# Batch attention in a fused kernel: four late output buffers instead of two, and the next stage's first rows normalised earlier at both joints

## The chip, the cores and the metric

The kernel runs on one NeuronCore of a Trainium2 chip. The metric is the device time of one launch in microseconds (us); the lower the better. The core has five engines that run their own instruction streams and meet only at semaphores: TensorE (PE, matmuls and transposes), VectorE (DVE), ScalarE (ACT), GpSimd (POOL) and SyncE (SP, which here issues every DMA).

## The reference, cut to what matters

Six layers run one after the other on x of 16 sequences by 512 rows by 256 columns. The first three (expert feed-forward, dilated attention, expert feed-forward) are not touched. The last three are a channel mix, an attention across the batch, and the channel mix again:

```python
x = x + 0.5 * channel_mix(layernorm(x))
x = x + batch_attention(layernorm(x))
x = x + 0.5 * channel_mix(layernorm(x))

def channel_mix(x):                      # 16 sequences, 512 x 256
    x_prev = shift_down_one_row(x)
    xr = mu_r * x + (1 - mu_r) * x_prev
    xk = mu_k * x + (1 - mu_k) * x_prev
    return sigmoid(xr @ W_r.T) * (square(relu(xk @ W_k.T)) @ W_v.T)

def batch_attention(x):
    q, k, v = x @ Wq.T, x @ Wk.T, x @ Wv.T
    scores = q @ k.reshape(b, d, s) / sqrt(d)
    attn = softmax(scores, axis=0)       # over the 16 sequences
    return where(tril, attn, 1e-9) @ v
```

## The kernel before, in words

The three last layers are one block of code, `mix_and_attend`: channel mix c1, batch attention b1, channel mix c2. Each engine gets one long instruction stream with all three, written out by hand, and nothing but semaphores orders the engines. So at a joint between two stages the order of the lines in each engine's stream decides what waits for what.

A "row" n of a channel mix is one sequence, 512 x 256 floats or 512 KB, held as 4 tiles of 128 rows; there are 16. c1 keeps five buffers of input (`RING`), two of output. For each row DVE takes mean and variance (`statistics`, or `front` in c2), POOL makes the reciprocal root (`root`), the row is scaled (in c1 and c2 by ACT, in b1 by DVE's `scale`), and PE transposes it (`turn_h`). In c1 DVE then runs `mixed`, `square` and `output` and PE runs `keys`, `receptance`, `values`. `output` writes first "rk" and then "y"; PE's `values(n)` waits for "rk" of row n-1, since both use one bank of PSUM.

The joint c1 to b1. Near the end of c1's loop on SP, at turn n == B - 2 = 14 and so behind the store of row 13, `open_sync` of b1 issues the load of b1's row 0, the weights, rows 1 and 2 and three constants. On DVE the loop of c1 ends with `square(15)`, `output(14)`. Then come b1's `open_vector` (two memsets, `statistics(0)`, `scale(0)`, `weight(0)`, `turned(0)`, `statistics(1)`) and c1's `output(15)`. PE, after `receptance(15)`, runs b1's `turn_h(0)`, then c1's `values(15)`, then b1's `query(0)`, `key(0)`, `turn_h(1)`. ACT turns the transposed row into its upper half (`turned`, L1984), DVE subtracts to get the lower (L2055).

b1 has a first part (16 rows: queries, keys, values), ten score blocks (`weigh` on DVE and POOL), and 32 output groups (`outputs` on PE, `output` on DVE, L2140). A group is 128 query rows of two sequences, 128 x 512 floats, 256 KB. The list `groups` has query block 3 (groups 0 to 7), block 2 (8 to 15), the first five of block 1 (16 to 20), and then blocks 0 and 1 mixed: group 21 is block 0, sequences 0 and 1; 22 is block 0, sequences 2 and 3; 23, 26 and 29 are block 1; the rest block 0. For each group DVE waits for the matmuls (a ring of four PSUM slots), for the residual `xo` read back from x_c, and for the store that last used its `yt` buffer. It adds and writes `yt`. SP's `put` then stores `yt` and at once loads the residual of group n + 2 into the `xo` buffer just freed. There are two buffers of each kind, so the residual of group n is asked for only when group n - 2 is done. PE's `outputs(n)` waits for DVE's output n - 4. Groups of block 0 also wait for POOL's `gather(1, g)` of the same sequences (L2038), which waits for PE's group of block 1 of these.

The joint b1 to c2. Behind store 17, SP issues c2's identity, mu and three weights (`load_weights`). Behind store 23 come c2's rows 0 and 1 (row 0 needs the landed store of group 21), behind 24 rows 2 and 3, behind 26 row 4. DVE runs outputs up to 25, `rests`, `front(0)`, outputs 26 and 27, `weight(0)`, `front(1)`, outputs 28 and 29, `mixed(0)`, outputs 30 and 31, `weight(1)`, and then c2's `front(2)`, `mixed(1)`. PE runs `outputs` to 28, c2's `turn_h(0)`, outputs 29 to 31, `turn_h(1)`, `keys(0)`. POOL runs gathers 0 to 5 of block 1, `root(0)`, gather 6, `root(1)`, gather 7.

`at` is a list of six blocks of 16 x 128 floats a partition (the attention weights). Score block n uses `at[n % 6]`, so `at[4]` and `at[5]` hold blocks 4 and 5, both of query block 2. They are read for the last time in the outputs of groups 8 to 15.

Of the kernel before, what the change touches and what calls it, by code (L numbers as in the profile page):

```python
# [14 lines left out]
B, S, D = 16, 512, 256  # L15
# [764 lines left out]
def channel_mix(nc, sems, name, src, dst, w, prior=None):  # L780

    stage = Stage()
    with ExitStack() as ctx:
        m = Memory(nc, ctx, name, sems)
# [59 lines left out]
        def sync(sp, after=None):  # L844
            for n in range(B):
                if after and n == B - 2:
                    after.open_sync(sp)
                d_out.wait(sp, at_(n), "y")
                sp.dma_start(row_tiles(dst, at_(n)), yt[n % 2][:]).then_inc(s_st[n % 2].sem, 16)
                if n + RING < B:  # L850
                    load(sp, n + RING)
            for k in range(2):
                sp.wait_ge(s_st[k].sem, 16 * (B // 2))
# [185 lines left out]
        def front(dve, n):  # L1039
            slot_wait(dve, s_ld, at_(n))  # L1040
            if n >= 2:
                a_h.wait(dve, at_(n - 2))
            norm.statistics(dve, at_(n))
# [48 lines left out]
        def vector(dve, after=None):  # L1092
            front(dve, 2)
            for n in range(B):
                if n + 1 < B:
                    mixed(dve, n + 1)
                square(dve, n)
                if n + 3 < B:
                    front(dve, n + 3)
                if n:  # L1100
                    output(dve, n - 1)
            if after:
                after.open_vector(dve)
            output(dve, B - 1)
# [589 lines left out]
def batch_attention(nc, sems, name, src, dst, w, prior):  # L1694

    stage = Stage()
    with ExitStack() as ctx:
# [18 lines left out]
        at = [m.sbuf(f"at{j}", B, P) for j in range(AT)]  # L1716
        yt = [m.sbuf(f"yt{k}", GB, D) for k in range(2)]
        q_blk = m.sbuf("q_blk", B, DC, P)
        mx, rc, rt = (m.sbuf(k, P) for k in ("mx", "rc", "rt"))
# [3 lines left out]
        tri, fill, unseen = (m.sbuf(k, P) for k in ("tri", "fill", "unseen"))  # L1723
        xo = [m.sbuf(f"xo{k}", GB, D) for k in range(2)]
        norm = Norm(m, NB, lambda t: xt[t.step % 3], half)
        p_s = m.psum("p_s", B, P)
# [12 lines left out]
        s_q = [m.track(f"s_q{k}", inc=16) for k in range(4)]  # L1739
        s_x, s_y = ([m.sem(f"s_{n}{k}") for k in range(2)] for n in "xy")  # L1740
        t_hT, a_hT, d_hT = m.track("t_hT"), m.track("a_hT"), m.track("d_hT")
# [17 lines left out]
        group_of = {group: n for n, group in enumerate(groups)}  # L1759
        HB = B // 2  # L1760

        def rows_of(a, n):
            qb, g = groups[n]
            return a.rearrange("(b s) d -> s b d", b=B)[qb * P:(qb + 1) * P, g * GB:(g + 1) * GB, :]
# [5 lines left out]
        def load_x(sp, n):  # L1770
            sp.dma_start(xo[n % 2][:], rows_of(src, n)).then_inc(s_x[n % 2], 16)

        def stored(sp, row):
            n = group_of[0, row // GB]
            sp.wait_ge(s_y[n % 2], 16 * (n // 2 + 1))

# [10 lines left out]
        def sync(sp, after):  # L1787
# [20 lines left out]
            def put(some):  # L1808
                for n in some:
                    d_y.wait(sp, at_(n))  # L1810
                    sp.dma_start(rows_of(dst, n), yt[n % 2][:]).then_inc(s_y[n % 2], 16)
                    if n + 2 < NB * G:
                        load_x(sp, n + 2)

            queries_for(2)
# [6 lines left out]
            after.load_weights(sp)  # L1822
            put(range(18, 24))
            after.load(sp, 0)
            after.load(sp, 1)
            put(range(24, 25))
            after.load(sp, 2)
# [3 lines left out]
            put(range(27, NB * G))  # L1831
            for k in range(2):
                sp.wait_ge(s_y[k], 16 * (NB * G // 2))

# [234 lines left out]

        def open_vector(dve):  # L2070
            dve.memset(unseen[:], UNSEEN).then_inc(s_z, 1)
            dve.memset(half[:], -0.5).then_inc(s_z, 1)
            statistics(dve, 0)
            scale(dve, 0)
            weight(dve, 0, wq)
            turned(dve, 0)
            statistics(dve, 1)

        def vector(dve, after):
# [54 lines left out]
            def output(some):  # L2134
                for n in some:
                    t_o.wait(dve, at_(n))
                    dve.wait_ge(s_x[n % 2], 16 * (n // 2 + 1))
                    if n >= 2:
                        dve.wait_ge(s_y[n % 2], 16 * (n // 2))
                    d_y.mark(dve.tensor_tensor(yt[n % 2][:], p_o[:, n % RING], xo[n % 2][:], ALU.add))  # L2140

# [12 lines left out]
            after.clear(dve)  # L2154
            output(range(18, 26))
            after.rests(dve)
            after.front(dve, 0)
            output(range(26, 28))
            after.weight(dve, 0)
            after.front(dve, 1)  # L2160
            output(range(28, 30))
            after.mixed(dve, 0)
            output(range(30, NB * G))
            after.weight(dve, 1)

    stage.stored, stage.scores_read, stage.outputs_read = stored, scores_read, outputs_read
    stage.open_sync, stage.open_tensor, stage.open_vector = open_sync, open_tensor, open_vector
# [110 lines left out]
```

## Time and profile before

| what | us |
|---|---|
| median of 3 runs (4042.88 to 4046.23) | 4043.06 |
| the profiled execution's own time | 4039.7 |
| its span, first to last instruction | 4037.8 |
| PE busy in it | 3821.2 (95%) |
| DVE / ACT / POOL busy in it | 3203.9 / 3070.6 / 2280.1 |
| mean granted TensorE clock (1 is full) | 0.984 |

The times at the start of rows below are us from the span's start. A row of a timeline gives start, length, engine, line, operation, what it writes and reads, how many instructions were merged, and in brackets how long the engine stood idle before it and what ended that. c1 ends and b1 begins near 3510; b1 ends and c2 begins near 3870.

### The profile page before, as it was taken

Reading aid. Unit: us, or ns where it says so; the run is one execution under the profiler, and the core shown is the slowest. Engines: PE = TensorE matmul, PEld = TensorE weight load, DVE = VectorE, ACT = ScalarE, POOL = GpSimd, SP = SyncE. Lnnn points to the kernel's source line nnn. Section 1 sums busy time; section 2 is a strip of 40 time slices with the busy share of each in tenths; the row PEclk is TensorE's granted clock in tenths of the full one; section 3 lists DMA queues with packets and bytes.
Section 4 is the critical chain, followed back from the end, with each engine's and each line's share of the span. In section 5 each row is a group of like instructions: output and inputs, shape, how many; then the busy total and the mean of one; then the engine's idle time right before and its main releaser. Section 6 shows DMA issues by size and latency. Waiting matters only on the chain. (4 is left out here: it accounts for less than half of the span.)

```text
span 4037.8 us, 82429 instructions
## 1 busy us (share of the span) xinstructions
PE 3821.2 (95%) x29464; PEld 3342.0 (83%) x29464; DVE 3203.9 (79%) x7740; ACT 3070.6 (76%) x7818; POOL 2280.1 (56%) x1818
## 2 busy tenths in 40 slices
PE   7999999999889999999998799999999988999989
PEld 6888888888768888888887688888888877898878
DVE  7888888888668787878876788888888867756567
ACT  6888888888678888888886688888888867632166
POOL 7888888888611111111100788888888866512356
PEclk8999999999989999999999899999999998999999
DMA  2000000000010000000000200000000002331342
GB/s 65 16 17 17 17 17 17 17 17 17 21 37 12 23 13 23 12 23 12 23 7 12 70 17 17 17 17 17 17 17 17 17 16 93 124 101 58 123 147 89
DMA packets 135064, 141.99 MB, mean 35 GB/s; under 512 B 8672, under 2 KB 131968, under 8 KB 134656
## 3 DMA queue, kind: packets, MB, share of 16 engines
q1 hardware_dynamic: 134656, 136.71, 10.6%
q8 instruction: 236, 3.87, 0.4%
q14 instruction: 172, 1.41, 0.1%
HBM read 80.06 MB, written 56.62 MB: 34 GB/s over the span
## 5 line engine op out<-in xcount | busy, mean ns | idle before, releaser
L300 POOL TENSOR_TENSOR f_grid<-f_sim 128x1024 f32<-128x1024 f32 x512 | 968.5, 1908 | 0.0
L1483 ACT ACTIVATE a_ex<-a_p_s,a_mneg 128x128 f32<-128x128 f32 x2048 | 726.4, 408 | 149.9 <-DVE a_mneg L1537 149.9
L686 DVE SCALAR_TENSOR_TENSOR f_p_u<-f_grid,f_te,f_p_dot 128x1024 f32<-128x1024 f32 x512 | 652.9, 1275 | 112.6 <-PE f_p_dot L106 66.1
L308 POOL TENSOR_TENSOR f_q<-f_q 128x1024 f32<-128x1024 f32 x256 | 607.2, 2383 | 123.1 <-ACT f_q L558 120.6
L695 DVE SCALAR_TENSOR_TENSOR f_q<-f_p_u,f_rz,f_grid 128x1024 f32<-128x1024 f32 x512 | 650.5, 1270 | 0.4
L539 ACT ACTIVATE f_grid<-f_grid,f_negm 128x1024 f32<-128x1024 f32 x512 | 559.5, 1143 | 0.0
L1483 ACT ACTIVATION_READ_ACCUMULATOR a_ex<-a_p_s,a_mneg 128x1 f32 x2048 | 507.2, 248 | 0.0
L443 PE MATMUL f_p_y<-f_eup,f_wT 128*128 128x256 f32 x2048 | 472.9, 379 | 0.0
L438 PE MATMUL f_p_y<-f_wdn,f_hs 128*128 128x256 f32 x2048 | 468.3, 382 | 0.0
L443 PEld LDWEIGHTS f_p_y<-f_eup,f_wT 128*128 128x128 f32 x2048 | 388.6, 190 | 57.6
L438 PEld LDWEIGHTS f_p_y<-f_wdn,f_hs 128*128 128x128 f32 x2048 | 378.9, 190 | 49.5
L1263 POOL TENSOR_TENSOR a_xb<-a_xt,a_bos 128x256 f32<-128x256 f32 x64 | 45.1, 736 | 577.3 <-DVE a_yt L1575 567.6
L1537 DVE TENSOR_REDUCE a_mneg<-a_p_s 128x4 f32<-128x512 f32 x512 | 330.3, 663 | 4.8 <-PE a_p_s L1337 4.8
L1543 DVE COPY a_exT<-a_p_s 128x512 f32<-128x512 f32 x384 | 261.0, 683 | 80.6 <-PE a_p_s L1348 79.1
L425 PE MATMUL f_p_wT<-f_ident,f_q 128*128 128x128 f32 x2048 | 269.2, 274 | 21.8 <-POOL f_q L308 20.4
L425 PEld LDWEIGHTS f_p_wT<-f_ident,f_q 128*128 128x128 f32 x2048 | 229.2, 141 | 44.3 <-POOL f_q L308 34.6
L552 ACT ACTIVATE f_hs<-f_p_hid 128x512 f32<-128x512 f32 x256 | 151.7, 593 | 141.6 <-PE f_p_hid L106 140.8
L1348 PE MATMUL a_p_s<-a_ident,a_ex 128*128 128x128 f32 x1536 | 244.5, 283 | 10.2 <-ACT a_ex L1483 4.8
L558 ACT ACTIVATE f_q<-f_q 128x2048 f32<-128x2048 f32 x128 | 244.3, 1908 | 0.0
L287 POOL TENSOR_TENSOR f_cand<-f_tx,f_ty 128x512 f32<-128x512 f32 x128 | 136.8, 1069 | 148.8 <-DVE f_ty L650 148.6
L1348 PEld LDWEIGHTS a_p_s<-a_ident,a_ex 128*128 128x128 f32 x1536 | 167.7, 141 | 56.5 <-ACT a_ex L1483 40.1
L546 ACT COPY f_wT<-f_p_wT 128x512 f32<-128x512 f32 x256 | 148.3, 579 | 76.5 <-PE f_p_wT L425 76.5
(622 smaller groups left out, 10448.3 us busy)
## 6 DMA issues: line engine op xcount, KB each, us to landing
x_f<-f_yt SPq DMA_DIRECT2D x64, 256.0 KB, 2.2
f_xt<-x SPq DMA_DIRECT2D x32, 256.0 KB, 2.9
a_xt<-x_f SPq DMA_DIRECT2D x16, 512.0 KB, 3.9
x_a<-a_yt SPq DMA_DIRECT2D x16, 512.0 KB, 2.9
f_xt<-x_a SPq DMA_DIRECT2D x32, 256.0 KB, 2.9
c_xt<-x_f SPq DMA_DIRECT2D x16, 512.0 KB, 4.9
x_c<-c_yt SPq DMA_DIRECT2D x16, 512.0 KB, 3.2
b1p_xt<-x_c SPq DMA_DIRECT2D x16, 512.0 KB, 3.9
```

What stands on the lines that cost most here:

```text
L300: g_grid.mark(pool.tensor_tensor(grid[v][:, hd, :].rearrange("p (i j) -> p i j", i=XROWS), sx[:, hd, :].unsqueeze(2).to_broadcast([P, XROW ...
L308: g_pair.mark(pool.tensor_tensor(q[v][:, 2 * k, :], q[v][:, 2 * k, :], q[v][:, 2 * k + 1, :], ALU.add), f"{v}{k}")
L425: last = pe.matmul(p_wT[:, e, :], q[v][:, hd, (k * HALF + e) * P:(k * HALF + e + 1) * P], ident[:], is_transpose=True, start=hd == 0, stop ...
L438: pe.matmul(p_y[:, v, :], hs[t.step % 2][:, e, v * P:(v + 1) * P], wdn[:, e, :], start=e == 0, stop=False)
L443: last = pe.matmul(p_y[:, v, :], wT[v][:, e, :], eup[:, e, :], start=False, stop=e == EC - 1)
L539: a_exp.mark(act.activation(grid[v][:, hd, :], grid[v][:, hd, :], ACT.Exp, bias=negm[:, v, hd:hd + 1]), f"{v}{hd}")
L686: d_mask.mark(dve.scalar_tensor_tensor(out=p_u[:], in0=grid[v][:, hd, :], scalar=te[:, v, hd, TOP - 1:TOP], in1=p_dot[:], op0=ALU.is_ge, o ...
L695: d_mul.mark(dve.scalar_tensor_tensor(out=q[v][:, hd, :], in0=p_u[:], scalar=rz[:, v, hd:hd + 1], in1=grid[v][:, hd, :], op0=ALU.mult, op1 ...
L1348: last = pe.transpose(p_e[i][:, n, :], ex[t.step % 2][:, i, n, :], ident[:])
L1483: last = act.activation(ex[t.step % 2][:, i, n, :], p_s[i][:, n, :], ACT.Exp, bias=mneg[:, i, n:n + 1], accum_out=z[t.step % 2][:, i, n:n ...
L1537: d_max.mark(dve.tensor_reduce(mneg[:, i, :], p_s[i][:], AX.X, ALU.max, negate=True), str(i))
L1543: d_ex.mark(dve.tensor_copy(exT[t.step % 2][:, i, :, :], p_e[i][:]), str(i))
```

## The change: what it does

It has three parts. First, two more buffers for outputs (`yt`) and two more for residuals (`xo`) are laid in the halves of `at[4]` and `at[5]`. Groups 0 to 15 use two buffers as before; from group 16 (`WIDE`) on, group n uses buffer n % 4. Behind the store of group 15 SP loads the residuals of 17, 18 and 19, and from 16 on the residual of n + 4. Second, at the joint of c1 and b1 `open_sync` runs one turn of SP earlier (behind the store of row 12), and the memsets, `statistics(0)` and `scale(0)` move on DVE ahead of c1's `output(14)`, as `first_row`. Third, at the joint of b1 and c2 SP asks for c2's rows 0 and 1 behind store 22 instead of 23, and for rows 2 and 3 behind store 24 as before. DVE runs `rests` behind output 23, `front(0)` behind 24, `weight(0)` and `front(1)` behind 26, `mixed(0)` behind 29 as before.

```diff
@@ channel_mix, sync
-                if after and n == B - 2:
+                if after and n == B - 3:
                     after.open_sync(sp)
@@ channel_mix, vector
                 if n + 3 < B:
                     front(dve, n + 3)
+                if after and n == B - 1:
+                    after.first_row(dve)
                 if n:
                     output(dve, n - 1)
@@ batch_attention
+        yt += [at[4][:, 4 * k:4 * k + 4].rearrange("p (g x) s -> p g (x s)", g=GB) for k in range(2)]
+        xo += [at[5][:, 4 * k:4 * k + 4].rearrange("p (g x) s -> p g (x s)", g=GB) for k in range(2)]
-        s_x, s_y = ([m.sem(f"s_{n}{k}") for k in range(2)] for n in "xy")
+        s_x, s_y = ([m.sem(f"s_{n}{k}") for k in range(4)] for n in "xy")
+        WIDE = 2 * G
+        buffer = [n % 2 if n < WIDE else n % 4 for n in range(NB * G)]
+        uses = [buffer[:n].count(buffer[n]) for n in range(NB * G)]
         def stored(sp, row):
             n = group_of[0, row // GB]
-            sp.wait_ge(s_y[n % 2], 16 * (n // 2 + 1))
+            sp.wait_ge(s_y[buffer[n]], 16 * (uses[n] + 1))
             def put(some):
                 for n in some:
                     d_y.wait(sp, at_(n))
-                    sp.dma_start(rows_of(dst, n), yt[n % 2][:]).then_inc(s_y[n % 2], 16)
-                    if n + 2 < NB * G:
+                    sp.dma_start(rows_of(dst, n), yt[buffer[n]][:]).then_inc(s_y[buffer[n]], 16)
+                    if n < WIDE:
                         load_x(sp, n + 2)
+                    if n == WIDE - 1:
+                        load_x(sp, n + 3)
+                        load_x(sp, n + 4)
+                    if WIDE <= n < NB * G - 4:
+                        load_x(sp, n + 4)
-            put(range(18, 24))
+            put(range(18, 23))
             after.load(sp, 0)
             after.load(sp, 1)
-            put(range(24, 25))
+            put(range(23, 25))
             after.load(sp, 2)
             after.load(sp, 3)
-        def open_vector(dve):
+        def first_row(dve):
             dve.memset(unseen[:], UNSEEN).then_inc(s_z, 1)
             dve.memset(half[:], -0.5).then_inc(s_z, 1)
             statistics(dve, 0)
             scale(dve, 0)
+
+        def open_vector(dve):
             weight(dve, 0, wq)
             turned(dve, 0)
             statistics(dve, 1)
@@ batch_attention, vector, end
             after.clear(dve)
-            output(range(18, 26))
+            output(range(18, 24))
             after.rests(dve)
+            output(range(24, 25))
             after.front(dve, 0)
-            output(range(26, 28))
+            output(range(25, 27))
             after.weight(dve, 0)
             after.front(dve, 1)
-            output(range(28, 30))
+            output(range(27, 30))
             after.mixed(dve, 0)
             output(range(30, NB * G))
             after.weight(dve, 1)
```

The waits in `load_x`, `output` and at the end of `sync` are changed in the same way to `buffer` and `uses`.

## Rows read from the trace of the kernel before

**Rows 1.** Timeline of VectorE at the joint of c1 and b1.
```profile
3504.06 1.22 DVE L1069 TENSOR_TENSOR c_ks<-c_relu,c_p_k 128x1024 f32<-128x1024 f32 x1 [4.17 <-ACT c_relu L1001]
3506.46 1.23 DVE L1076 SCALAR_TENSOR_TENSOR c_rk<-c_p_v,c_rs 128x1024 f32<-128x1024 f32 x1 [1.18 <-PE c_p_v L936]
...
3508.92 0.17 DVE L2071 MEMSET b_unseen<- 128x128 f32 x1
...
3510.51 0.38 DVE L128 BATCH_NORM_AGGREGATE b_mv<-b_bs 128x2 f32<-128x6 f32 x4
3512.43 1.38 DVE L145 TENSOR_SCALAR b1p_h<-b1p_xt,b_mv,b_rstd 128x256 f32<-128x256 f32 x4 [1.53 <-POOL b_rstd L137]
3513.73 0.68 DVE L2068 TENSOR_TENSOR b1p_wql<-b_q_blk,b1p_wqh 128x512 fp32r<-128x512 f32 x1
3516.98 1.22 DVE L2055 TENSOR_TENSOR b1p_hT0l<-b_p_s,b1p_hT0h 128x1024 fp32r<-128x1024 f32 x1 [2.57 <-ACT b1p_hT0h L1984]
```
**Rows 2.** Timeline of TensorE at the same joint.
```profile
3513.95 1.94 PE L1841 MATMUL b_p_s<-b_ident,b1p_h 128*128 128x128 f32 x8 [4.73 <-DVE b1p_h L145]
3515.69 4.14 PE L936 MATMUL c_p_v<-c_wv,c_ks 128*128 128x256 f32 x16
...
3523.02 0.39 PE L104 MATMUL b_p_o<-b1p_wkl,b1p_hT0h 128*128 128x256 f32 x1 [0.45 <-DVE b1p_wkl L2068]
```
**Rows 3.** SyncE's DMA issues: when b1's first row was asked for.
```profile
3500.33 0.51 SPq L1768 DMA_DIRECT2D b1p_xt<-x_c  x1
```
**Rows 4.** Waits from 3820 to 3890: us in total, times, longest us.
```profile
DVE b_yt L2140 <- DMA b_xo<-x_c: 23.6, 12, 5.1
```
**Rows 5.** Windows: PE, PEld, DVE, ACT, POOL busy (count); PE clock, DMA share, GB/s.
```profile
3834.00:3839.00 5.00, 2.95 (x14) 2.27 (x12) 0.00 (x0) 0.62 (x1) 2.69 (x3) 1.00 0.96 307
3851.00:3859.00 8.00, 1.98 (x10) 1.81 (x10) 2.43 (x9) 2.07 (x4) 2.93 (x5) 0.73 1.06 363
```
**Rows 6.** SyncE's DMA issues near the joint of b1 and c2.
```profile
3833.33 0.47 SPq L1771 DMA_DIRECT2D b_xo<-x_c  x1
...
3834.45 0.92 SPq L1771 DMA_DIRECT2D b_xo<-x_c  x1
...
3846.65 1.07 SPq L825 DMA_DIRECT2D c_xt<-x_b  x2
```
**Rows 7.** Timeline of VectorE at that joint.
```profile
3839.00 0.69 DVE L2140 TENSOR_TENSOR b_yt<-b_p_o,b_xo 128x512 f32<-128x512 f32 x1 [5.07 <-DMA b_xo<-x_c]
3840.32 0.69 DVE L2140 TENSOR_TENSOR b_yt<-b_p_o,b_xo 128x512 f32<-128x512 f32 x1 [0.62 <-DMA b_xo<-x_c]
...
3850.95 1.41 DVE L124 BATCH_NORM_STATS2 c_bs<-c_xt 128x6 f32<-128x256 f32 x4 [0.72 <-DMA c_xt<-x_b]
...
3864.07 0.74 DVE L1060 SCALAR_TENSOR_TENSOR c_xk<-c_p_tr,c_mu,c_oldk 128x512 f32<-128x512 f32 x1
...
3868.41 0.69 DVE L2140 TENSOR_TENSOR b_yt<-b_p_o,b_xo 128x512 f32<-128x512 f32 x1 [1.02 <-DMA b_xo<-x_c]
3869.02 1.65 DVE L1052 TENSOR_TENSOR c_wrl<-c_raw,c_wrh 128x512 fp32r<-128x512 f32 x1
```
**Rows 8.** Timelines of TensorE, GpSimd and ScalarE at that joint.
```profile
3857.22 1.94 PE L899 MATMUL c_p_tr<-c_ident,c_h 128*128 128x128 f32 x8 [6.02 <-issue]
...
3862.81 0.59 PE L1943 MATMUL b_p_o<-b_v_all,b_at 128*128 128x256 f32 x2
...
3866.02 0.67 PE L1943 MATMUL b_p_o<-b_v_all,b_at 128*128 128x256 f32 x2 [1.32 <-POOL b_v_all L2038]
...
3864.60 1.27 POOL L2038 TENSOR_TENSOR b_v_all<-b_v_all 128x512 f32<-128x512 f32 x1
...
3866.66 1.03 ACT L995 CAST c_xk0h<-c_xk 128x1024 fp32r<-128x1024 f32 x1
```
**Rows 9.** DMA issues: KB each, us to landing; c2's first load alone.
```profile
c_xt<-x_b SPq DMA_DIRECT2D x1, 512.0 KB, 4.3
```
**Rows 10.** The chain that ended last: PE's transposes of c2's third row.
```profile
3878.48 1.93 PE c_p_tr L899 x8
```

More of the change, by code:

```diff
@@ L1770, in load_x @@
         def load_x(sp, n):
-            sp.dma_start(xo[n % 2][:], rows_of(src, n)).then_inc(s_x[n % 2], 16)
+            sp.dma_start(xo[buffer[n]][:], rows_of(src, n)).then_inc(s_x[buffer[n]], 16)
         def stored(sp, row):
             n = group_of[0, row // GB]
-            sp.wait_ge(s_y[n % 2], 16 * (n // 2 + 1))
+            sp.wait_ge(s_y[buffer[n]], 16 * (uses[n] + 1))
         def open_sync(sp):
@@ L1831, in sync @@
             put(range(27, NB * G))
-            for k in range(2):
-                sp.wait_ge(s_y[k], 16 * (NB * G // 2))
+            for k in range(4):
+                sp.wait_ge(s_y[k], 16 * buffer.count(k))
         def turn_h(pe, n):
@@ L2136, in output @@
                     t_o.wait(dve, at_(n))
[L2137 to L2140, printed above, removed]
+                    dve.wait_ge(s_x[buffer[n]], 16 * (uses[n] + 1))
+                    if uses[n]:
+                        dve.wait_ge(s_y[buffer[n]], 16 * uses[n])
+                    d_y.mark(dve.tensor_tensor(yt[buffer[n]][:], p_o[:, n % RING], xo[buffer[n]][:], ALU.add))
             for n in range(5):
@@ L2164, in vector @@
             after.weight(dve, 1)
-    stage.stored, stage.scores_read, stage.outputs_read = stored, scores_read, outputs_read
+    stage.stored, stage.scores_read, stage.outputs_read, stage.first_row = stored, scores_read, outputs_read, first_row
     stage.open_sync, stage.open_tensor, stage.open_vector = open_sync, open_tensor, open_vector
```

## The prediction

> **What bounds the kernel now.** I read the page first: PE is busy 95% of the span, so only moments when PE waits can be won. The chain that ended last runs through PE almost everywhere in the last three stages, and leaves it at two places, the two joints that the change touches. I then read each joint on the timelines of DVE, PE, SP, POOL and ACT, and the windows for the DMA share.
>
> At the first joint PE stands 4.73 us until DVE has scaled b1's first row [rows 2]. On DVE the reader is to see an idle 1.18 us behind `square(15)`, then `output(14)`, and only then the memset that opens b1 at 3508.92 [rows 1]. Row 0 had been asked for at 3500.33 [rows 3] and was there: the memset and the statistics stand back to back behind `output(14)`.
>
> At the second joint DVE waited 12 times and 23.6 us in all for residuals [rows 4]. These waits look like the price of two buffers: a residual is asked for only when the output two groups before is done. But the windows say something else as well. From 3834 to 3839 the 16 DMA engines are at a share of 0.96, from 3851 to 3859 at 1.06 [rows 5]. For much of the joint the transfers wait for each other, not for a buffer. So the 23.6 us are no measure of the gain; what ends last is c2's row 0, which lands just before 3850.95 [rows 7].
>
> **First joint, step by step.** Asking for row 0 one turn earlier (one row of c1, about 10 us) costs SP ten issues in a stretch where it waits for DVE anyway; it stands ahead of store 13, which is not due for another 10 us. Cost nothing; without that cover, some 0.5 us an issue [rows 3], so 5 us, and onto a store nobody waits for.
>
> `first_row` can start when `square(15)` ends, at 3504.06 + 1.22 = 3505.28, so 3.65 us before 3508.92 [rows 1]. Statistics, POOL's root and the scale follow as before, with POOL idle at that time: the scaled row is ready at 3510.15 and not 3513.81. PE's transposes start then (its `receptance(15)` ends at 3509.2: 3513.95 less the idle 4.73 [rows 2]), ACT's upper half and DVE's `turned(0)` follow. Now what it is moved past: `output(14)` takes DVE 2.46 us (3506.46 to 3508.92) and starts at 3510.15. With `weight(0)` (0.6 to 0.7) it fills DVE until 3513.3. `turned(0)` stood at 3516.98 and can come at 3516.98 - 3.65 = 3513.33 [rows 1]. So `output(14)` lies just inside the hole in which DVE waited for ACT (2.57) and in the old 1.53 wait for POOL, less the 1.18 it had in front. Behind it waits PE's `values(15)`, for "rk" of row 14, written at about 3511.4. The transposes end between 3511.2 (at their usual 0.9 to 1.0) and 3512.1 (at the 1.94 of the row), so 0.2 us or nothing is lost there, and PE has slack, because `key(0)` waits for DVE (0.45) [rows 2]. Gain: 3.65 us. Bounds: 3.0 if "rk" and the queue on DVE cost more than the hole, 4.5 if PE, which now idles one us and not 4.73, doesn't run its transposes and `values(15)` slowly (4.14 for the latter [rows 2], 3.45 as usual) and that reaches the path.
>
> **Second joint.** Residuals 18 and 19 are now asked for behind store 15, before 3815, when nothing else is moving. Groups 16 to 19 therefore pass at once, and 20 and 21 take over the places of 18 and 19 in SP's order. The weights come behind store 17 in both kernels. So the residual loads issued at 3833.33 and 3834.45 [rows 6] are those of 22 and 23 and no longer of 20 and 21, and they land when they did, near 3838.95 and 3840.3, when DVE could take its two outputs [rows 7]. This is the backlog that four buffers don't shorten. The gain in groups is two.
>
> After that the backlog goes on where before it ran dry. A 256 KB transfer costs 0.65 us in it (one store and one load between the two outputs, 1.32 us [rows 7]); at the 363 GB/s of [rows 5] 262 KB take 0.72. I take 0.7. SP issues store 20, load 24, store 21, load 25 in one go behind load 23, as their outputs were done by 3834. In order they land at 3841.0, 3841.7, 3842.4 and 3843.1. Output 22 is at 3838.95, so store 22 and load 26 are issued by 3840.6. Then SP stands in `load(0)` until store 21 has landed: 3842.4, and issues c2's row 0 at 3842.45, before it was 3846.65 [rows 6]. Ahead of it are load 25, store 22, load 26 (2.1 us), so it is there at 3844.5 + 1.4 = 3845.9 at the earliest; with the 4.3 us it took before [rows 9], at 3846.75. I take the later: `front(0)` starts 4.2 us earlier than 3850.95. DVE is free by then (output 24 is done near 3842.5). What is queued behind `front(0)` on DVE are outputs 25 and 26 with residuals that landed long before. They wait some 4 us for nothing; their stores and loads 29 and 30 come later by that, and land by 3857, before PE has group 29.
>
> From `front(0)` the chain to PE's `turn_h(0)` is POOL's root, ACT's scale, 6.27 us [rows 7, 8]: 3853.0 in place of 3857.22. PE stands as before, some 6 us. Group 29 then is ready at 3858.6 (3862.81 less 4.2 [rows 8]). Here a second wait goes. POOL's last gather started at 3864.60, behind `root(1)`, though group 29 was ready at 3862.81; and PE's group 31 waited 1.32 for it [rows 8]. Now `front(1)` stands ahead of outputs 27 to 29, so `root(1)` is over by 3855, the gather starts at 3858.65, ends at 3859.9, and PE goes straight on. Group 31 starts at 3866.02 - 4.2 - 1.32 = 3860.5, so it is 5.5 us earlier. On DVE `mixed(0)` comes behind output 29, at 3859.3 (before 3864.07), output 31 at 3862.6 (before 3868.41), `weight(1)` at 3863.3 (before 3869.02): 5.7. ACT's cast of xk0 depends on `mixed(0)` and no longer on the scale of row 1: 3861.3, before 3866.66, so 5.35 [rows 7, 8]. The join of both, PE's `turn_h(2)` at 3878.48 [rows 10], moves by the smaller. From there PE runs row on row, and the gain reaches the end. I take 5.4 us. Bounds: row 0 landing at 3845.9 gives 6.2; landing as late as before leaves only the 1.3 of the gather.
>
> **Rule and row.** The Trainium skill ("DMA: Bandwidth & Descriptors", section Specifications) puts HBM at about 358 GB/s for one core, and the trace at 363 GB/s agrees, hardly above it. By that rule 256 KB take 0.73 us and the sum hardly moves. The same page (Queues, rings and completion order) says descriptors are consumed in ring order, but that completion isn't strictly in order between issues. If the transfers were shared and not served in order, load 22 would be held up by the four transfers now issued behind it; what this gives is the first rival.
>
> **The sum.** 3.65 + 5.4 = 9.05 us. The profiled execution took 4039.7, so it would take 4030.7, span 4028.8. It was 3.4 under the median of the runs, so I set the difference against the median: 4043.06 - 9.05 = 4034.0. The parts between the joints issue the same instructions; two loads move into an empty time of the DMA engines.
>
> **The rivals.** *The DMA engines eat the second gain.* At shares of 0.96 to 1.06 a deeper queue only makes each transfer wait longer. If row 0 lands at 3851 in spite of the earlier issue, the second joint gives 1.3 and the sum is 4.95: 4038.1. For it: those shares. Against: the share is low between 3839 and 3841, when SP had only just been given new work, and row 0 lies behind a fixed number of bytes. Chance 0.22. *The first joint gives nothing:* `output(14)` behind `scale(0)` holds PE's `values(15)` and `turned(0)` as long as the earlier start saves. It would need 3.65 us where I count 0.2. The sum is 5.4: 4037.7. Chance 0.10. *The change does nothing,* since waits elsewhere take it back: 4043. Chance 0.07. *Slower:* `front(0)` at the head of DVE's queue waits for a row that itself waits for store 21 in a full queue; outputs 25 on, and PE's group 29, stand behind it. Each us of row 0's landing costs one. The other gains (3.65 and 1.3) are gone when it lands at 3855.9, and over 0.2% are lost at 3864. That needs 13 to 21 us from issue to landing, where the row shows 4.3. 4052. Chance 0.03.
>
> **How the numbers follow.** A measurement of this kernel can tell about 0.2%, 8.1 us, from no change. My forecast, 4034.0, is just past it; its own range is 4030.5 to 4037 (joint sums 12.5 to 6: the bounds of both joints, and 1 us of scatter), with a chance of 0.58, and about a tenth of the whole lies in that range but under 8.1 us. Faster by over 0.2%: 0.52, within: 0.44, slower: 0.04. The range, to hold 8 in 10, takes in the first two rivals: 4030 to 4039.5.
>
> **What would show it.** In the trace of the changed kernel: PE's idle before L1841 at the first joint at one us, the memset right behind `square(15)`, `output(14)` behind the scale, and `key(0)` 3.65 us earlier. At the second joint: no wait before outputs 18 and 19, a wait of over 4 us before output 22, no row under a share of 0.8 from 3829 to 3850, L825's first issue near 3842.5 - 3.65 and `front(0)` 4.2 us + 3.65 earlier than 3850.95, PE's group 31 with no wait for POOL. I am wrong if row 0 takes over 6 us to land, or if `turn_h(1)` and `keys(0)` wait for something that I didn't list.

## The result, and the profile after

| | kernel before | changed kernel |
|---|---|---|
| median of 8 runs, us | 4043.62 (4037.59 to 4047.96) | 4032.12 (4027.77 to 4038.89) |
| span of the profiled execution, us | 4037.8 | 4027.7 |
| ratio of the runs | | 0.9972, 95% interval 0.9962 to 0.9983 |

The changed kernel is 0.28% faster: 4043.62 x 0.0028 = 11.3 us, 6.9 to 15.4 by the interval. The two profiled executions differ by 10.1 us. Forecast were 9.05 us and 4034.0.

The first joint on VectorE after the change, beside [rows 1]:

```profile
3504.14 1.22 DVE L1069 TENSOR_TENSOR c_ks<-c_relu,c_p_k 128x1024 f32<-128x1024 f32 x1 [4.17 <-ACT c_relu L1001]
3505.34 0.17 DVE L2083 MEMSET b_unseen<- 128x128 f32 x1
...
3509.18 1.38 DVE L145 TENSOR_SCALAR b1p_h<-b1p_xt,b_mv,b_rstd 128x256 f32<-128x256 f32 x4 [1.54 <-POOL b_rstd L137]
3510.47 1.22 DVE L1076 SCALAR_TENSOR_TENSOR c_rk<-c_p_v,c_rs 128x1024 f32<-128x1024 f32 x1
3511.72 1.23 DVE L1081 TENSOR_TENSOR c_yt<-c_rk,c_xt 128x1024 f32<-128x1024 f32 x1
3512.87 0.69 DVE L2080 TENSOR_TENSOR b1p_wql<-b_q_blk,b1p_wqh 128x512 fp32r<-128x512 f32 x1
3513.47 1.22 DVE L2067 TENSOR_TENSOR b1p_hT0l<-b_p_s,b1p_hT0h 128x1024 fp32r<-128x1024 f32 x1
```

The memset stands right behind `square(15)`. `output(14)` comes behind the scale, and with `weight(0)` it ends just when `turned(0)` can start: the row of L2067 has no idle time in front of it, where the row before had 2.57. On TensorE, beside [rows 2]:

```profile
3510.70 1.06 PE L1853 MATMUL b_p_s<-b_ident,b1p_h 128*128 128x128 f32 x8 [1.39 <-DVE b1p_h L145]
3511.84 3.69 PE L936 MATMUL c_p_v<-c_wv,c_ks 128*128 128x256 f32 x16
3519.51 0.39 PE L104 MATMUL b_p_o<-b1p_wkl,b1p_hT0h 128*128 128x256 f32 x1 [1.22 <-DVE b1p_wkl L2080]
```

TensorE idles 1.39 us and not 4.73, and its transposes take 1.06 and not 1.94, since the clock no longer falls: granted were 0.50 from 3514 to 3516 before, and 1.00 from 3510.5 to 3512 now. But it then waits 1.22 for VectorE before `key(0)`, where it waited 0.45: the faster matmuls bring nothing, as VectorE sets the pace.

At the second joint, VectorE after the change, beside [rows 7]:

```profile
3824.76 0.69 DVE L2154 TENSOR_TENSOR b_at<-b_p_o,b_at 128x512 f32<-128x512 f32 x1
...
3829.70 0.69 DVE L2154 TENSOR_TENSOR b_yt<-b_p_o,b_xo 128x512 f32<-128x512 f32 x1 [1.19 <-DMA b_xo<-x_c]
3834.90 0.69 DVE L2154 TENSOR_TENSOR b_at<-b_p_o,b_at 128x512 f32<-128x512 f32 x1 [4.51 <-DMA b_at<-x_c]
...
3842.37 1.41 DVE L124 BATCH_NORM_STATS2 c_bs<-c_xt 128x6 f32<-128x256 f32 x4 [4.02 <-DMA c_xt<-x_b]
...
3853.90 0.69 DVE L2154 TENSOR_TENSOR b_yt<-b_p_o,b_xo 128x512 f32<-128x512 f32 x1 [4.42 <-PE b_p_o L1955]
3854.51 0.74 DVE L1060 SCALAR_TENSOR_TENSOR c_xk<-c_p_tr,c_mu,c_oldk 128x512 f32<-128x512 f32 x1
...
3858.34 2.28 DVE L1052 TENSOR_TENSOR c_wrl<-c_raw,c_wrh 128x512 fp32r<-128x512 f32 x1
```

Where `b_at` stands as an output or a second input, it is one of the new buffers. Outputs 18 and 19 have no wait. The long wait (4.51) is still there; it now stands before output 22, two groups further on. `front(0)` starts at 3842.37, 8.58 us earlier, of which some 3.5 come from the first joint. The chain that ended last shows what held row 0 (start, us, what):

```profile
3832.93 5.36 DMA x_b<-b_yt
3838.29 0.02 issue
3838.30 0.36 SPq L825
```

SyncE issues store 21 at 3832.93, then load 25, store 22 and load 26, and stands at L825, c2's first load, until store 21 has landed behind the backlog. The windows (last three columns: PE clock, DMA share, GB/s), beside [rows 5]. First the one in which the DMA engines of the kernel before had little to do:

```profile
3839.00:3841.00 2.00, 1.25 (x6) 1.12 (x7) 1.37 (x2) 0.00 (x0) 0.00 (x0) 1.00 0.37 123
```

Then three of the changed kernel:

```profile
3834.00:3839.00 5.00, 5.00 (x25) 4.41 (x24) 2.15 (x4) 0.14 (x1) 0.84 (x1) 1.00 1.09 383
3839.00:3841.00 2.00, 2.00 (x11) 1.77 (x10) 0.00 (x0) 0.00 (x0) 0.00 (x0) 1.00 0.87 289
3841.00:3845.00 4.00, 1.99 (x10) 1.40 (x8) 2.53 (x10) 0.00 (x0) 0.51 (x2) 1.00 0.88 246
```

From 3839 to 3841 the share is now 0.87 and not 0.37, and from 3834 to 3839 the DMA engines move 383 GB/s. Cut into stretches of 1 us two dips are left in the changed kernel, a share of 0.49 from 3830 to 3831 and of 0.63 from 3842 to 3843. The Trainium skill ("DMA: Bandwidth & Descriptors", section Specifications) puts HBM at about 358 GB/s for one core; here the measurement, 383 GB/s over 5 us, is above it.

On TensorE and GpSimd, beside [rows 8]:

```profile
3848.70 1.94 PE L899 MATMUL c_p_tr<-c_ident,c_h 128*128 128x128 f32 x8 [5.71 <-issue]
3857.37 1.07 PE L899 MATMUL c_p_tr<-c_ident,c_h 128*128 128x128 f32 x8
3868.43 1.60 PE L899 MATMUL c_p_tr<-c_ident,c_h 128*128 128x128 f32 x8 [2.33 <-ACT c_h L978]
...
3853.95 1.28 POOL L2050 TENSOR_TENSOR b_v_all<-b_v_all 128x512 f32<-128x512 f32 x1 [3.91 <-PE b_p_o L1955]
```

TensorE still stands 5.71 us before `turn_h(0)`. Between it and the second transposes there is no wait in brackets any more: the last gather now waits for TensorE (3.91) and no longer TensorE for the gather. The third transposes are at 3868.43, before at 3878.48 [rows 10].

### The profile page after: what moved, and what is told of

Same layout as the page of the kernel before. It is cut to its first block and busy times, and to the rows that moved or that the text cites. A ratio compares the mean times of both kernels' runs of the same rounds, so it can differ in the third digit from the quotient of the medians.

```text
span 4027.7 us, 82430 instructions
## 1 busy us (share of the span) xinstructions
PE 3816.6 (95%) x29464; PEld 3337.1 (83%) x29464; DVE 3206.9 (80%) x7740; ACT 3074.0 (76%) x7818; POOL 2282.1 (57%) x1818
## 3 DMA queue, kind: packets, MB, share of 16 engines
q8 instruction: 235, 3.85, 0.4%
## 5 line engine op out<-in xcount | busy, mean ns | idle before, releaser
L1350 PE MATMUL a_p_s<-a_ident,a_ex 128*128 128x128 f32 x1536 | 243.8, 282 | 10.7 <-ACT a_ex L1485 4.8
```

The costliest lines, as they stand in the source:

```text
L1350: last = pe.transpose(p_e[i][:, n, :], ex[t.step % 2][:, i, n, :], ident[:])
```

## The experiments

A single time of this kernel scatters by several us, more than a joint is worth. So most kernels were judged by two yardsticks, each read from a single trace. The first runs from the start of `square(15)` on VectorE to the start of `key(0)` on TensorE. The second runs from VectorE's output 16 (the first row of L2154 behind the last score block) to TensorE's third transposes in c2. Beside the second stand two marks on the way: when c2's row 0 is asked for and when `front(0)` starts, both from output 16. Each number below is a difference of two starts, in us.

| kernel | first | row 0 asked | front(0) | second | square(15) to output 16 |
|---|---|---|---|---|---|
| before | 18.96 | 19.64 | 23.94 | 51.47 | 322.95 |
| changed | 15.37 | 14.77 | 18.84 | 44.90 | 319.39 |
| changed, again | 15.36 | 15.13 | 19.82 | 47.05 | 321.07 |
| first joint only | 15.37 | 20.16 | 25.15 | 52.32 | 321.06 |
| second joint only | 20.01 | 15.01 | 19.51 | 46.45 | 325.47 |
| four buffers, old order | 15.36 | 14.15 | 20.11 | 46.76 | 320.88 |
| two buffers, new orders | 15.36 | 16.54 | 21.68 | 51.08 | 321.06 |
| two buffers, new orders, again | 15.36 | 17.12 | 22.12 | 53.31 | 321.06 |
| first_row, old requests | 15.36 | 19.29 | 24.10 | 51.53 | 319.36 |
| mu in one load | 15.36 | 14.23 | 18.13 | 44.70 | 319.35 |
| weights late | 15.36 | 12.86 | 16.97 | 41.66 | 321.03 |
| eight residual buffers | 15.35 | 11.90 | 16.86 | 41.42 | 321.04 |
| all three | 15.36 | 9.57 | 14.27 | 41.18 | 320.89 |
| all three, value weights last | 15.36 | 9.69 | 16.20 | 40.77 | 320.91 |

**First joint only.** The kernel before with these lines:

```diff
-                if after and n == B - 2:
+                if after and n == B - 3:
                     after.open_sync(sp)
...
+                if after and n == B - 1:
+                    after.first_row(dve)
                 if n:
                     output(dve, n - 1)
```

> Only the first joint's part is kept: the earlier requests of SyncE and first_row ahead of output(14). Two yardsticks are read from each trace. The first runs from the start of square(15) to the start of key(0) on TensorE: 18.96 us in the kernel before, 15.37 in the changed one. The second runs from VectorE's output 16 to TensorE's transposes of c2's third row: 51.47 and 44.90. My theory is that the two joints are independent: the first yardstick reads 15.4, the second stays at 51.5, and the kernel is 3.6 us (0.09%) faster than before, which the runs can hardly tell from nothing. The rival that the first joint gives its time back inside b1 or at the second joint has the second yardstick above 52.5 or the span less than 2 us shorter.

Measured: 15.37 and 52.32; 4037.57 us against 4040.45 for the kernel before on the same chip, ratio 0.9992 (0.9983 to 1.0001). The first yardstick reads 15.4 whether the second joint is changed or not. By time alone it can't be told from nothing, as expected.

**Second joint only.** The changed kernel with the first joint back as it was:

```diff
-                if after and n == B - 3:
+                if after and n == B - 2:
                     after.open_sync(sp)
...
-                if after and n == B - 1:
-                    after.first_row(dve)
...
         def open_vector(dve):
+            first_row(dve)
```

> Only the second joint's part is kept (four buffers, c2's rows asked for one group sooner, VectorE's new order); the first joint is as before. Theory: first yardstick 18.96, second 44.9, kernel 6.6 us (0.16%) faster. The rival is that the two parts only work together: the second yardstick above 46.

Measured: second yardstick 46.45; 4035.67 us against 4040.45, ratio 0.9989 (0.998 to 0.9999), so 4.4 us, 0.4 to 8.1. It is over the 46 that I had set for the rival, but the changed kernel taken again (below) gave 47.05, so this limit was too tight for a single trace. What stands is that each half works without the other. The first yardstick, expected at 18.96, is 20.01 with the same code at that joint: behind the same wait of 4.73 us `values(15)` took 5.21 us and not 4.14.

**Four buffers, old order.** The changed kernel with the stores, c2's loads and VectorE's order as before:

```diff
-            put(range(18, 23))
+            put(range(18, 24))
             after.load(sp, 0)
             after.load(sp, 1)
-            put(range(23, 25))
+            put(range(24, 25))
...
-            output(range(18, 24))
+            output(range(18, 26))
             after.rests(dve)
-            output(range(24, 25))
             after.front(dve, 0)
-            output(range(25, 27))
+            output(range(26, 28))
             after.weight(dve, 0)
             after.front(dve, 1)
-            output(range(27, 30))
+            output(range(28, 30))
```

> The changed kernel with the old order at the second joint: SyncE asks for c2's rows 0 and 1 behind store 23 and VectorE runs front(0) behind output 25, as before the change; the four buffers stay. My theory is that the buffers carry most of the second joint: output 22 still comes 4 us earlier than two buffers allow, row 0 is asked for about when output 23 is done, so perhaps 1 us later than in the changed kernel, and the second yardstick is 46 to 48 (3.5 to 5.5 of the 6.57 us are left). The rival, that the order does it (row 0 asked for sooner, GpSimd's last gather no longer held), has it above 49.5.

Measured: 46.76, inside the theory's range and inside the scatter of the changed kernel itself. Row 0 was asked for at 14.15, not later than in the changed kernel, though it stands one store further back, and took 6.0 us until `front(0)`. TensorE's waits from 3826 to 3880 (us in total, times, longest):

```profile
PE c_p_tr L899 <- issue: 7.0, 1, 7.0
PE c_p_tr L899 <- ACT c_h L978: 2.4, 1, 2.4
PE c_p_k L104 <- POOL c_xk0l L868: 1.8, 1, 1.8
PE b_p_o L1955 <- DVE b_yt L2154: 1.0, 1, 1.0
```

No wait for GpSimd's gather (`b_v_all`) is left, although the order is the old one. With four buffers outputs 26 and 27 don't wait for residuals, so `front(1)` comes early enough by itself (here at 3850.03, 8.6 us before the last gather's start at 3858.61).

**Two buffers, new orders.** The kernel before with `first_row`, the earlier requests and the new orders at the second joint, that is the diff above read the other way:

```diff
-            put(range(18, 24))
+            put(range(18, 23))
             after.load(sp, 0)
             after.load(sp, 1)
-            put(range(24, 25))
+            put(range(23, 25))
...
```

> Both joints' new orders with two buffers only. Row 0 is then asked for behind store 22, at 3843.8 in the trace of before where it was 3846.65 (less the 3.6 us of the first joint), but the residuals of 25 on are asked for behind it. Theory: row 0 lands 1.5 to 2.5 us sooner, the last gather is no longer held, late residuals cost some of it again: second yardstick 48 to 50.5. The rival, that the order is all that counts, has 45 to 46.

Measured: `front(0)` 2.3 us sooner than before, as expected, but the second yardstick at 51.08, outside both theories. In this trace eight of the twelve matmuls of keys(0) ran at half clock, so I took it again.

> The kernel with two buffers and the new orders once more, unchanged. Its second yardstick was 51.08, with the first matmuls of keys(0) at 0.43 us each where other traces have 0.23. Theory: that is TensorE's clock, which comes back at a different moment in each execution, and the orders alone are worth more; front(0) is again 21.5 to 22 us behind output 16 and the yardstick is 49 to 51. Rival: the new orders with two buffers always end at 51.

Measured: 53.31; `front(0)` at 22.12. My theory fell: neither trace is below the old order's 51.5 to 52.3 by more than the scatter. VectorE in the second trace, output 28 and output 29:

```profile
3859.96 0.69 DVE L2144 TENSOR_TENSOR b_yt<-b_p_o,b_xo 128x512 f32<-128x512 f32 x1 [0.68 <-DMA b_xo<-x_c]
3864.03 0.69 DVE L2144 TENSOR_TENSOR b_yt<-b_p_o,b_xo 128x512 f32<-128x512 f32 x1 [3.38 <-DMA b_xo<-x_c]
3864.64 0.74 DVE L1060 SCALAR_TENSOR_TENSOR c_xk<-c_p_tr,c_mu,c_oldk 128x512 f32<-128x512 f32 x1
```

With two buffers, output 29 waits 3.38 us for its residual, and c2's `mixed(0)` stands behind it. TensorE's second transposes in turn wait for `mixed(0)`:

```profile
3867.50 1.07 PE L899 MATMUL c_p_tr<-c_ident,c_h 128*128 128x128 f32 x8 [2.90 <-DVE c_xr L1060]
...
3870.36 0.76 PE L104 MATMUL c_p_k<-c_xk0l,c_wkh 128*128 128x512 f32 x1 [1.79 <-POOL c_xk0l L868]
```

This wait was 1.81 us in the first of the two traces and stands in none of the old order. keys(0) was again at half clock, this time all twelve matmuls (granted 0.50); it took 5.25 us, 4.42 in the first trace, and 2.87 at full clock, as in every trace with the old order. From the second to the third transposes the two traces take 12.4 and 13.3 us where the others but one have 10.7 to 11.1, so some 1.4 and 2.2 us of the 51.08 and 53.31 are the clock's. Whether the orders bring this on, by the wait just ahead of it, or whether it was chance, two traces don't show.

**The changed kernel again,** with no edit.

> The changed kernel once more, unchanged, for the scatter of the yardsticks. From square(15) to output 16 the traces so far read 319.4 or 321.0 us, with no relation to the edits; I expect one of these two values again, and 44.5 to 46.5 for the second yardstick, front(0) within 0.5 us of 18.84. If front(0) is off by more than 1 us, the single readings of the edits above mean little.

Measured: 321.07, 47.05 and 19.82. The same code reads 2.15 us apart on the second yardstick and 1.0 on `front(0)`. Single readings that differ by less than that are not told apart here. The last pair of kernels below reads 1.9 apart on `front(0)` with the same code up to there, so for that mark alone 2 us is the safer limit.

**first_row with the old requests.** The kernel before with `first_row` alone; `open_sync` stays at n == B - 2.

> The kernel before with first_row ahead of output(14), but SyncE asks for b1's row 0 as late as before (3500.33; that load took 4.9 us to land in the trace of before, so 3505.2, and the statistics want it at 3505.4). Theory: the earlier requests are a safety only, the first yardstick (square(15) to key(0)) is 15.4 to 16.0. The rival, that the earlier requests are needed, has it above 16.5. Second yardstick as before, 51.5 to 52.5.

Measured: 15.36. Row 0 is asked for at 3497.74 and the memset, with the statistics behind it, starts at 3502.67 with no wait:

```profile
3497.74 0.51 SPq L1770 DMA_DIRECT2D b1p_xt<-x_c  x1
...
3502.67 0.17 DVE L2073 MEMSET b_unseen<- 128x128 f32 x1
3502.76 0.42 DVE L124 BATCH_NORM_STATS2 b_bs<-b1p_xt 128x6 f32<-128x256 f32 x1
```

The load took 4.7 us, so the row had landed at 3502.4, 0.2 us before it was wanted. The earlier requests gained nothing in this execution.

**mu in one load.** The host lays the two vectors out as [128, 2, 2]:

```diff
-                for n, k in enumerate(("mu_k", "mu_r")):
-                    sp.dma_start(mu[:, n, :], w[k].rearrange("(c p) -> p c", p=P)).then_inc(s_mu, 16)
+            sp.dma_start(mu[:], w["mu"]).then_inc(s_mu, 16)
```

> The changed kernel with the two mu vectors laid out on the host in the order in which they are used, so one load of 128 pieces of 16 bytes in place of two with 256 pieces of 4 bytes each. In the trace of before, between the residuals at 3833.24 and 3838.95, five transfers of 256 KB and one of 64 KB explain 3.7 of 5.7 us; the rest should be mu. If the backlog of the DMA engines sets row 0's landing, front(0) starts 1 to 2 us sooner behind output 16 than the 18.84 us of the changed kernel, and the second yardstick is 43.3 to 44.3. The rival, that row 0 waits for buffers or for the matmuls, has front(0) at 18.5 or later.

Measured: `front(0)` at 18.13, 0.7 sooner than one trace of the changed kernel and 1.7 sooner than the other, and 44.70, above the 43.3 to 44.3 expected. Inconclusive.

**Weights late.** The changed kernel, each weight with a semaphore of its own and the last two loads taken out of `load_weights`:

```diff
             after.load(sp, 1)
+            after.load_weight(sp, 1)
             put(range(23, 25))
...
             after.load(sp, 4)
+            after.load_weight(sp, 2)
```

> The changed kernel with c2's receptance weights asked for behind its row 1 and the value weights behind row 4, 512 KB less in front of row 0. Backlog theory: front(0) starts 1.4 us sooner (17.4 behind output 16), second yardstick 43.5. Rival (buffers or matmuls): no sooner than 18.5. A risk: weight(1) on VectorE may wait for the weights, with the second yardstick then above 44.9 although front(0) is sooner.

Measured: `front(0)` at 16.97, 1.9 and 2.8 sooner than the two traces of the changed kernel, and 41.66, 3.2 and 5.4 sooner. Buffers and order are the same in both kernels, so it is the 512 KB less in front of row 0 that let it land sooner; by the scatter of `front(0)` the amount is only roughly known.

**Eight residual buffers.** The changed kernel with

```diff
                     if n == WIDE - 1:
-                        load_x(sp, n + 3)
-                        load_x(sp, n + 4)
-                    if WIDE <= n < NB * G - 4:
+                        for ahead in range(3, 9):
+                            load_x(sp, n + ahead)
+                    if WIDE + 4 <= n < NB * G - 4:
                         load_x(sp, n + 4)
```

> The changed kernel with eight residual buffers (all the rest of at[4] and at[5]): behind store 15 SyncE loads six more residuals (18 to 23) into the time when nothing moves, then none behind stores 16 to 19, and from store 20 on the one of n + 4 as before. So 1 MB less lies in front of c2's row 0 and outputs 22 and 23 don't stand behind the weights. Backlog theory: row 0 is asked for about 11 us and front(0) starts 15 to 16 us behind output 16 (18.84 in the changed kernel), second yardstick 41 to 42.5, and less of TensorE's idle time ahead of its transposes. Rival (four buffers took all there was): front(0) at 18 or later.

Measured: row 0 asked for at 11.90, `front(0)` at 16.86, 41.42: half of what I expected for `front(0)`, all of it for the yardstick. VectorE's waits:

```profile
3833.67 0.69 DVE L2157 TENSOR_TENSOR b_yt<-b_p_o,b_at 128x512 f32<-128x512 f32 x1 [1.35 <-PE b_p_o L1958]
3837.29 1.39 DVE L2157 TENSOR_TENSOR b_at<-b_p_o,b_at 128x512 f32<-128x512 f32 x2 [2.93 <-DMA x_b<-b_at]
```

No output waits for a residual; output 22 waits 2.93 for store 18, whose output buffer it needs and which stands behind the weights. The wait has moved to the other four buffers.

In both of these kernels the second yardstick gains more than `front(0)`. The rest is TensorE's clock. From `front(0)` to TensorE's first transposes every kernel takes 6.3 us. From the first to the second transposes the four-buffer kernels with the changed kernel's weights and residuals, and the one with mu in one load, take 8.7 to 9.8 us, with the transposes at 1.94 and a granted clock of 0.82 (changed) or 0.72 (changed, again), behind 5.0 to 7.0 us of idle time. The kernels with the weights late or with eight residual buffers idle 3.85 and 3.73 us there, are granted 1.00, and take 7.3 and 7.2. So a row 0 that lands 2 us sooner here gave 1.4 to 2.7 us more through the clock.

**All three edits.** The changed kernel with the last three diffs together.

> The changed kernel with the last three edits together: mu in one load, the receptance and value weights behind c2's rows 1 and 4, eight residual buffers. Alone, they started front(0) 0.7, 1.9 and 2.0 us sooner behind output 16. Backlog theory: they add up where they take different bytes, so front(0) at 14.5 to 15.5 us and the second yardstick at 39 to 40.5 (44.9 in the changed kernel); the kernel is 15 us (0.37%, at least 0.25%) faster than before. The rival, that another wait takes over at once (stores that hold the four output buffers, or the matmuls of group 28, which end 19.3 us behind output 16), has front(0) at 16.5 or later or the second yardstick above 41.

Measured: `front(0)` at 14.27, the best of all and below what I expected, but the second yardstick at 41.18, where the rival had it. The waits of VectorE and TensorE that explain it:

```profile
3852.54 0.69 DVE L2164 TENSOR_TENSOR b_at<-b_p_o,b_at 128x512 f32<-128x512 f32 x1 [1.66 <-DMA b_at<-x_c]
3853.15 2.88 DVE L1056 TENSOR_TENSOR c_wrl<-c_raw,c_wrh 128x512 fp32r<-128x512 f32 x1
```

```profile
3843.27 1.06 PE L903 MATMUL c_p_tr<-c_ident,c_h 128*128 128x128 f32 x8 [1.15 <-issue]
3850.44 1.06 PE L903 MATMUL c_p_tr<-c_ident,c_h 128*128 128x128 f32 x8
3853.29 0.63 PE L104 MATMUL c_p_k<-c_xk0l,c_wkh 128*128 128x512 f32 x1 [1.79 <-POOL c_xk0l L872]
...
3863.85 1.97 PE L903 MATMUL c_p_tr<-c_ident,c_h 128*128 128x128 f32 x8 [3.18 <-ACT c_h L982]
```

TensorE's idle time ahead of `turn_h(0)` is down to 1.15 us. Output 31 now waits 1.66 for its residual, and eight matmuls of keys(0) ran at half clock (0.63 each; 0.40 at full). Timed, this kernel takes 4027.04 us against 4042.19 for the kernel before on the same chip, ratio 0.9965 (0.9951 to 0.9979), 14 us. It beats the kernel before. That it beats the changed kernel (0.9972) the runs don't show, as the intervals overlap.

**Value weights last.** The kernel with all three edits and

```diff
             after.load(sp, 4)
-            after.load_weight(sp, 2)
-            put(range(27, NB * G))
+            put(range(27, 29))
+            after.load_weight(sp, 2)
+            put(range(29, NB * G))
```

> The kernel with all three further edits, but the 256 KB of value weights are asked for behind store 28 instead of behind row 4, so behind the last residual but none. In the run with all edits, front(0) came at 14.27 us behind output 16 and TensorE's second transposes at 27.77, but the third ones only at 41.18, with output 31 waiting 1.66 us for its residual and TensorE at half clock in keys(0). Theory: with the value weights out of the way output 31 doesn't wait, and the second yardstick is 38.5 to 40.5 where the clock stays up, 41 where it falls once more; 1 us less in the span than with all edits, too little for the runs to tell. The rival: the wait for the residual stays, since load 31 is held by something else than the weights, and the yardstick is 41 again at full clock.

Measured: output 31 doesn't wait and keys(0) is at full clock, yet 40.77, above the 38.5 to 40.5 expected, since `front(0)` was at 16.20, 1.9 us later than in the run before with the same code up to there. Row 0 was asked for at 9.69 after output 16 (9.57 there) and took that much longer. 4028.03 us against 4042.66, ratio 0.9966 (0.9953 to 0.9978). Load 31 took 6.4 us and not 7.4, so by these two traces the value weights had held it for about 1.0 us. That is less than the wait of 1.66: the rest is gone because VectorE came to output 31 later in this trace. The gain of moving the value weights drowns in the scatter.

## Why the prediction was right

**First joint.** Forecast 3.65 us, measured 18.96 - 15.37 = 3.59. The 15.4 is the same in every kernel with `first_row`; the old code read 18.96 and, in the kernel with the second joint only, 20.01, so the gain was 3.6 or 4.6 us, depending on how long TensorE's clock stayed down behind the 4.73 us wait (`values(15)` took 1.07 us longer in the second). The prediction named this in its upper bound of 4.5. The steps held one by one: the memset behind `square(15)`, 1.39 us of idle TensorE (forecast "one us"), `output(14)` inside the holes, nothing lost by `values(15)`. The rival of the first joint giving nothing is excluded. The cost of the moved requests is nothing, as forecast; that they brought nothing either I had not asked.

**Second joint.** Forecast 5.4 us. The traces with two buffers and the old order read 51.47, 52.32 and 51.53, mean 51.77; the three with the full second part 44.90, 46.45 and 47.05, mean 46.13: 5.6. The pair of profiles shown with the result reads 6.57, the luckiest of the three; this one us makes its 10.1 in place of 9.05. The steps held: the long wait moved from output 20 to output 22 (forecast 3838.95 less the first joint's 3.65, so 3835.3; measured 3834.90), the DMA engines had a share of 0.87 and more in windows of 2 to 5 us (in single us it fell to 0.49 and 0.63 once each), SyncE stood at `load(0)` for store 21 (forecast 3838.8, measured 3838.30), `front(0)` at 3842.37 (forecast 3843.1).

**Two sizes were off and cancelled.** Split at `front(0)`, with the mean of the same three traces on either side, the 5.6 us are 24.40 - 19.39 = 5.0 up to it and 0.6 behind it. Forecast were 4.2 and 1.2. Row 0 came sooner than I had it, and the wait for the last gather was worth less: it had been 1.32 us in the trace that I read, but was 0.80 and 0.74 in the two others with the old order and two buffers, and TensorE's half clock behind `turn_h(0)` moves this stretch by over 1 us. That the sum of 5.4 fits so well is luck in part.

**One term was put down to the wrong part.** I gave 1.3 of the 5.4 us to the new order on VectorE, since it puts `front(1)` and so `root(1)` ahead of the last gather. With four buffers and the old order this wait is gone as well and the yardstick is 46.76, 5.0 of the 5.6 us and within the scatter of all of it. With two buffers and the new orders it is 51.08 and 53.31, no better than before; keys(0) at half clock makes some 1.4 and 2.2 us of these. So the total was right because the buffers carry it. What the orders do alone: `front(0)` comes 2 us sooner, and the late residuals take most or all of it back.

**The rivals.** That the DMA engines eat the gain was the right worry with the wrong consequence: they are the bound, and the weights and residuals taken out of row 0's way move it by 2 to 3 us each, but the earlier place in the queue counts in full. The slower rival needed row 0 to take 13 us; it took 4.0, and 4.7 and 4.5 in the two other traces with this second joint.

**A sum that doesn't come out.** The prediction's own range was to be the bounds of both joints and 1 us of scatter. These bounds add up to 3.0 + 1.3 = 4.3 and 4.5 + 6.2 = 10.7 us, with the scatter 3.3 to 11.7, and not the 6 to 12.5 that it gives. The measured 11.3 us lie inside either.

**What stays open.** Whether the orders are worth anything on top of four buffers: one trace (46.76) against three (44.90 to 47.05) can't say. Whether keys(0) at half clock belongs to the orders with two buffers or was chance. And what mu costs.

## What to carry to other kernels

When an engine waits on transfers and the DMA share in that window is near 1, count the bytes that stand in the queue ahead of the transfer that ends last, not the waits. Buffers pay here because they move two residuals into a time when nothing moves and let the queue go on where it ran dry; moving weights that aren't needed yet out of the way gave another 3 to 5 us on the second yardstick on top of the four buffers, and it takes no buffer itself; with two buffers it wasn't tried. A transfer that lands sooner can pay twice, since the shorter wait may leave TensorE's clock up. And an operation of the next stage can go ahead of one of the last where the latter fits into a wait that the next stage has anyway: find the hole in the trace, add up what you put into it, and see who waits for its result.

## What the runs showed of the hardware

Between score block 4's matmuls and the first outputs TensorE waits 2.5 us in all fourteen traces. In four of them (before, changed, first_row with the old requests, mu in one load) the 64 matmul records behind it span 14.05 us, in the other ten 15.53 to 15.74. From the kernel with the first joint only, and then from the changed kernel:

```profile
3712.97 15.74 PE L1945 MATMUL b_p_o<-b_v_all,b_at 128*128 128x256 f32 x64 [2.50 <-issue]
```

```profile
3712.76 14.05 PE L1955 MATMUL b_p_o<-b_v_all,b_at 128*128 128x256 f32 x64 [2.50 <-issue]
```

The granted clock from 3700 to 3730 is 0.94 in these ten and 1.00 in the four, whatever the edit: after the same idle time the clock sometimes falls to the lower of its two levels (1.2 of 2.4 GHz) and sometimes doesn't. This is the 319.4 or 321.0 us in the last column of the table (322.95 and 325.47 where the first joint is as before, with its own scatter in it), 1.7 us of scatter from one wait. The waits of 4.73 us at the first joint and of 5.0 to 7.6 ahead of `turn_h(0)` at the second all cost the clock in these traces, but for how long it stays down varies too: the first yardstick of two kernels with the same code there is 18.96 and 20.01, with `values(15)` at 4.14 and 5.21 us. At the same two places waits of 1.15 and 1.39 us left it up; so did 3.08, 3.73 and 3.85 in three traces (value weights last, eight residual buffers, weights late), where the transposes behind them took 1.06. The length of the wait alone doesn't decide: ahead of keys(0) TensorE waits 1.8 us in all four-buffer kernels, and behind it the clock was down in one of them (all three edits, granted 0.66 from 3853 to 3858) and up in the others.

The landing time of one 512 KB load behind nearly the same queue was 4.7 us in one trace and 6.5 in another (all three edits, with and without the value weights moved, which lie behind it).
